# A two-layer decoder's attention phase: probabilities turned as half-height tiles ahead of the scores, and one score matmul for two key sets

## The reference

```python
q = (layernorm(x) @ wq + bq) / 8            # 16 heads x 64
k = concat(ctx @ wk + bk, mk)               # 128 token keys + 128 memory keys
v = concat(ctx @ wv + bv, mv)
x = x + softmax(q @ k.T) @ v @ wo + bo      # per sequence and head, fp32
```

## Time and profile before

| | us |
|---|---|
| median of 3 timed runs | 1543.92 |
| lowest and highest | 1542.75, 1546.67 |
| profiled execution, span | 1569.9 |
| TensorE busy in the span | 1397.6 (89%) |
| VectorE busy | 1162.8 (74%) |
| ScalarE busy | 1103.5 (70%) |
| GpSimd busy | 604.5 (39%) |

### The profile page before, as it was taken

How to read it: one execution, slowest core, us unless ns; L and a number is a source line. 1 busy time by engine, 2 the same in 40 slices (tenths; PEclk the granted TensorE clock), 3 DMA queues, 4 the chain that set the end, 5 groups by cost and what they waited for, 6 DMA issues and landing times.

```text
span 1569.9 us, 42930 instructions
## 1 busy us (share of the span) xinstructions
PE 1397.6 (89%) x15465; PEld 1050.6 (67%) x15465; DVE 1162.8 (74%) x2779; ACT 1103.5 (70%) x2899; POOL 604.5 (39%) x679
## 2 busy tenths in 40 slices
PE   2358999999999999999895899989989999999995
PEld 0124777777777777777674799856666667776663
DVE  3999879898888979776466344456688888887665
ACT  1126999889888988988794466647666776876652
POOL 0002423353443424210103535446655655544452
PEclk9999999999999999999998899989999999999996
DMA  6644141332214231011012332230101010000000
GB/s 173 157 101 95 42 102 49 77 73 76 57 52 99 52 96 47 15 46 45 14 35 61 94 91 79 62 123 16 29 12 35 12 38 9 23 22 3 22 9 14
DMA packets 82317, 88.63 MB, mean 56 GB/s; under 512 B 15296, under 2 KB 71488, under 8 KB 77504
## 3 DMA queue, kind: packets, MB, share of 16 engines
q1 hardware_dynamic: 74496, 73.65, 18.2%
q0 software_dynamic: 4096, 8.40, 1.8%
q10 hardware_dynamic: 3520, 3.84, 0.7%
HBM read 64.89 MB, written 17.83 MB: 53 GB/s over the span
## 4 chain that ended last, share of the span: by engine, by line
PE 71%; DVE 16%; issue 7%; ACT 3%; DMA 1%; ACTq 1%; SPq 0%; another core or an unknown queue 0%; DVEq 0%
PE P L1981 9%; PE P L898 7%; PE P L760 7%; PE P L744 5%; PE P L1514 4%; PE P L1481 4%; PE P L2045 3%; PE P L1999 3%; PE P L880 3%; PE P L746 3%; PE P L857 3%; PE P L868 3%; PE P L852 3%; PE P L1943 2%; PE P L2069 2%
## 5 line engine op out<-in xcount | busy, mean ns | idle before, releaser
L950 ACT ACTIVATE pr<-P,nm 128x256 f32<-128x256 f32 x512 | 237.7, 489 | 10.2 <-DVE nm L1122 10.2
L2193 ACT ACTIVATE et<-P 128x1024 f32<-128x1024 f32 x128 | 131.2, 1025 | 101.1 <-PE P L1988 100.9
L1122 DVE TENSOR_REDUCE nm<-P 128x4 f32<-128x1024 f32 x128 | 156.1, 1220 | 53.0 <-PE P L746 47.7
L352 POOL TENSOR_TENSOR rstd<-ve,mhalf 128x1 f32<-128x1 f32 (+2 forms) x81 | 75.9, 939 | 255.7 <-DVE ve L347 252.9
L934 ACT COPY ptS<-P 128x512 f32<-128x512 f32 x256 | 137.0, 586 | 40.3 <-PE P L760 33.7
L760 PE MATMUL P<-ident,pr 128*128 128x128 f32 x1024 | 141.4, 281 | 7.3 <-issue 3.3
L925 ACT ACTIVATE pr<-pr,ri 128x256 f32<-128x256 f32 x256 | 118.7, 522 | 26.4 <-DVE pr L1099 25.0
L744 PE MATMUL P<-kt_w,qt 64*128 64x128 f32 x1024 | 127.6, 311 | 4.5 <-ACT pr L950 4.3
L1573 ACT ACTIVATE hT<-P,mixing 128x128 f32<-128x128 f32 x284 | 81.4, 368 | 66.7 <-PE P L1481 59.6
L760 PEld LDWEIGHTS P<-ident,pr 128*128 128x128 f32 x1024 | 111.0, 142 | 24.2 <-issue 11.1
L664 POOL TENSOR_TENSOR kv_qk<-kv_qk,r_w 128x512 f32<-128x512 f32 x48 | 61.1, 1272 | 161.9 <-DVE pr L1099 115.7
(11 more groups left out here) (355 smaller groups left out, 4039.8 us busy)
## 6 DMA issues: line engine op xcount, KB each, us to landing
kv_qk<-scr_v SPq DMA_DIRECT2D x16, 1024.0 KB, 8.1
r_w<-scr_r SPq DMA_DIRECT2D x16, 1024.0 KB, 10.7
xt<-scr_xs SPq DMA_DIRECT2D x71, 64.0 KB, 1.8
scr_ys<-yt SPq DMA_DIRECT2D x71, 64.0 KB
x<-in_x SPq DMA_DIRECT2D x8, 256.0 KB, 9.7
scr_v<-mixing SPq DMA_DIRECT2D x8, 256.0 KB, 2.0
scr_r<-mixing SPq DMA_DIRECT2D x8, 256.0 KB, 2.0
xb<-in_x SPq DMA_DIRECT2D x8, 256.0 KB, 4.3
```

The costliest lines, as they stand in the source:

```text
L950: e = nc.scalar.activation(pr[:, s % 3, h * KEYS:(h + 1) * KEYS], scores(s)[:, h // 2, (h % 2) * KEYS:(h % 2 + 1) * KEYS], ACT.Exp, bias=n ...
L1122: nc.vector.tensor_reduce(nm[:, s % 3, 0:4].rearrange("p (a h) -> p a h", a=2), scores(s).rearrange("p a (h k) -> p a h k", k=KEYS), AX.X, ...
L2193: nc.scalar.activation(et[:, u % 4, :, :, :], scoresT, ACT.Exp).then_inc(S["h_exp"], 1)
```

## The change

1. On TensorE the transposes of unit s - 2 now come before the scores of unit s.
2. Each 128x128 transpose becomes two of 64x128 (queries 0 to 63, queries 64 to 127). The first half of all eight goes to bank 4, the second half to bank 5; the two semaphore steps come with the last pair.
3. ScalarE's two copies follow: each copies one half of the queries for all eight key blocks, from 8 x 64 columns in the bank to eight pieces of 64 in `ptS`.
4. `KT`'s chunks get 128 columns more, which hold the memory keys; `mkT` becomes a view of them. One matmul with a moving operand of two pieces (128 columns of tokens, 128 of memory) takes the place of two.
5. The experts' second weights use the first 4,096 words of the larger buffer.

```diff
-        r8_w1, kt_w2, qt = [sb_shared(n, E * F) for n in ("r8_w1", "kt_w2", "qt")]
+        r8_w1, qt = [sb_shared(n, E * F) for n in ("r8_w1", "qt")]
+        kt_w2 = sb_shared("kt_w2", 8 * (N + MEM))
...
-            KT = kt_w2.rearrange("p (c n) -> p c n", n=N)
+            KT = kt_w2.rearrange("p (c n) -> p c n", n=N + MEM)
+            mkT = KT[:, :, N:N + MEM]
...
-                    if 0 <= s < UNITS:
-                        g, hq, b = unit(s)
...
-                        for cc in range(2):
-                            for hh in range(2):
-                                bank = scores(s)[:, hh, :]
-                                part, c = slice(64 * hh, 64 * hh + 64), 2 * hq + cc
-                                q = QT[part, c, b * T:(b + 1) * T]
-                                nc.tensor.matmul(bank[:, cc * KEYS:cc * KEYS + T], q, KT[part, c, b * T:(b + 1) * T],
-                                                 start=True, stop=True)
-                                m = nc.tensor.matmul(bank[:, cc * KEYS + T:(cc + 1) * KEYS], q, mkT[part, c, :],
-                                                     start=True, stop=True)
-                        m.then_inc(S["b_s"], 1)
-
                     i = s - LAG_PT
...
                         for kb in range(2):
                             for h in range(4):
-                                m = nc.tensor.transpose(P[:, 4 + kb, h * T:(h + 1) * T],
-                                                        pr[:, i % 3, h * KEYS + kb * T:h * KEYS + (kb + 1) * T],
-                                                        ident[:, :])
-                            m.then_inc(S["b_pt"], 1)
+                                k = 4 * kb + h
+                                for half in range(2):
+                                    part = slice(64 * half, 64 * half + 64)
+                                    m = nc.tensor.transpose(P[:, 4 + half, 64 * k:64 * k + 64],
+                                                            pr[part, i % 3, h * KEYS + kb * T:h * KEYS + (kb + 1) * T],
+                                                            ident[part, part])
+                                    if k == 7:
+                                        m.then_inc(S["b_pt"], 1)
+
+                    if 0 <= s < UNITS:
+                        g, hq, b = unit(s)
...
+                        for cc in range(2):
+                            for hh in range(2):
+                                part, c = slice(64 * hh, 64 * hh + 64), 2 * hq + cc
+                                keys = KT[part, c, :].rearrange("p (m k) -> p m k", k=T)[:, b:GS + 1:GS - b, :]
+                                m = nc.tensor.matmul(scores(s)[:, hh, cc * KEYS:(cc + 1) * KEYS], QT[part, c, b * T:(b + 1) * T],
+                                                     keys, start=True, stop=True)
+                        m.then_inc(S["b_s"], 1)
...
-                        for kb in range(2):
-                            act.wait_ge(S["b_pt"], 2 * i + kb + 1)
-                            nc.scalar.copy(ptS[:, i % 2, kb * 512:(kb + 1) * 512], P[:, 4 + kb, :])\
-                              .then_inc(S["b_pts"], 1)
+                        for half in range(2):
+                            act.wait_ge(S["b_pt"], 2 * i + half + 1)
+                            nc.scalar.copy(ptS[:, i % 2, :].rearrange("p (k q) -> p k q", q=T)[:, :, 64 * half:64 * half + 64],
+                                           P[:, 4 + half, :].rearrange("p (k q) -> p k q", q=64)).then_inc(S["b_pts"], 1)
```

More of the change, by code:

```diff
@@ L447, in first_phase @@
             bv = sb1("bv", [128, H * DK])
-            mkT = sb1("mkT", [128, 8, MEM])
             mv = sb1("mv", [128, H * DK])
@@ L647, in sync_program @@
                             e0, e1 = half * E // 2, (half + 1) * E // 2
-                            sp.dma_start(units_of(kt_w2)[:, e0 * FC:e1 * FC, :],
+                            sp.dma_start(units_of(kt_w2[:, 0:E * F])[:, e0 * FC:e1 * FC, :],
                                          d["w2T"].rearrange("(u f) h -> f u h", f=128)[:, e0 * FC:e1 * FC, :])\
@@ L759, in tensor_program @@
                             for h in range(4):
-                                m = nc.tensor.transpose(P[:, 4 + kb, h * T:(h + 1) * T],
-                                                        pr[:, i % 3, h * KEYS + kb * T:h * KEYS + (kb + 1) * T],
-                                                        ident[:, :])
-                            m.then_inc(S["b_pt"], 1)
+                                k = 4 * kb + h
[8 more added lines that the diff above has]
+                        g, hq, b = unit(s)
+                        pe.wait_ge(S["b_q"], 8 * g + 2 * hq + 2)
+                        pe.wait_ge(S["b_k"], 8 * g + 2 * hq + 2)
+                        if s:
+                            pe.wait_ge(S["b_exp"], 2 * s - 1)
+                        for cc in range(2):
[5 more added lines that the diff above has]
+                        m.then_inc(S["b_s"], 1)
                     g = group_at(s, BANK7["norm"])
@@ L1016, in scalar_program @@
                             act.wait_ge(S["b_kp"], 8 * g + c + 1)
-                            nc.scalar.activation(KT[:, c, :], P[:, 3, :], ACT.Identity, bias=bqk[:, 1, c:c + 1])\
+                            nc.scalar.activation(KT[:, c, 0:N], P[:, 3, :], ACT.Identity, bias=bqk[:, 1, c:c + 1])\
                               .then_inc(S["b_k"], 1)
@@ L1349, in sb2 @@
                 return own.enter_context(nc.sbuf_tensor(name, shape, dt))
-            w1, w2, b1, b2 = r8_w1, kt_w2, mixing[:, 0:E * D], mixing[:, 8 * N:8 * N + E * D]
+            w1, w2, b1, b2 = r8_w1, kt_w2[:, 0:E * F], mixing[:, 0:E * D], mixing[:, 8 * N:8 * N + E * D]
             qS, kS, vD, xb, ya, yb, xnD, xTd, qkv, qkq, hn3 = homes
```

## The result

| | before | changed |
|---|---|---|
| median, us | 1544.24 | 1581.57 |
| lowest, highest | 1542.75, 1546.67 | 1580.05, 1582.76 |
| span of the profiled execution | 1569.9 | 1578.3 |

The ratio is 1.023, with a 95% interval of 1.022 to 1.025: 37 us slower. The forecast was 1615 us, slower by 71. The direction and the mechanism were right, and the size was twice too large.

The account below looks back on a forecast made before the run. TensorE bounds the kernel, with VectorE and ScalarE having little to spare. The new loop adds 60 us in groups 1 to 5, then +9, +4 and -2: 1543.9 + 71 = 1615 us, range 1572 to 1656.

Parts of the forecast that it names:

- the loop: First phase: VectorE's add holds up transposes, scores, reduction, then the next add; +71 us, chance 0.73.
- VectorE's legs of group 3 plus sixteen TensorE legs: Group 3's time: reduction start to next add's end (67.8 us), plus sixteen times add's end to reduction start (2.25): 103.8.
- Transposes, 0.89 us: TensorE, each unit: eight half-height loads in each half, side by side, at 0.111 us each.
- Half time: Rival: half-height transposes on TensorE take half the time because 64 rows load twice as quickly; 1577 us, chance 0.09.
- Taking turns: Rival: the array's two halves load in turn, so TensorE's transposes take 1.78 us; 1695 us, chance 0.06.
- Faster, TensorE stays the bound: Rival: VectorE's add is done before TensorE's slot begins, so only 0.12 us a slot is saved; 1529 us, chance 0.09.
- The signs: Expected first-phase trace: 6.3 to 6.7 us a slot, 50 us or more TensorE idle, busy share about 0.86.
- Scores, 0.12 us: TensorE's score matmuls per slot: 0.09 us saved on a restart, 0.03 from fewer, wider steps.
- TensorE's saving: TensorE's block of scores and transposes goes from 2.12 to 2.0 us, 0.12 us a slot saved.
- Copies: nothing: ScalarE's two copies per unit, now in pieces with gaps, were taken to cost nothing; upper bound 19 us a group.
- Groups 0, 6 and 7: First phase's first and last two groups of sixteen slots: +9, +4 and -2 us.

Follow-up runs that it names:

- e3: Changed kernel with VectorE's add from bank 4 moved from the head of its next slot into the same slot; ratio 1.000 to before.
- e9: Changed kernel with half tiles turned by an ordinary fp32 matmul with the identity instead of transpose mode; 1763.3 us where before takes 1546.4.
- e6: Kernel before with only the 256-column score matmuls and mkT inside KT; old order, transposes and copies; ratio 0.9925 to before.
- e2: Changed kernel with the scores first again, half-height transposes behind them; ratio 0.981 to before, 1541.1 against 1572.3 us.
- e8: The changed kernel itself, unaltered, run again in a later session; ratio 1.024 to before.
- e4: Changed kernel with the scores first again and VectorE's add from bank 4 made early; ratio 0.987 to before.
- e5: Changed kernel, scores first, transposes behind the query or key projection, probabilities times values ahead of bank 4's projection; ratio 1.038 to before.
- e10: Changed kernel with scores first again and the recurrent block's additions moved from VectorE to GpSimd from group 2 on; ratio 0.981 to before.
- e12: Changed kernel with scores first and transposes behind the bank 7 work, ahead of the query or key projection; ratio 0.989 to before.
- e7: Kernel before with only the half-height transposes and their copies; old order and scores; ratio 0.9875 to before.

## Why the prediction was right, and where its size was off

- *What bounds the kernel; the loop.* Right. e1, with nothing but the order changed, is 6.8% slower; e3, with nothing but the add moved, takes the change's 2.4% back.
- *The rule "VectorE's legs of group 3 plus sixteen TensorE legs".* Right within 1.5 us for legs of 1.92 to 3.22 us: 98.5 against 97.99 (leg 1.92), 108.6 against 107.27 (2.55), 119.3 against 120.74 (3.22). Two legs always make up a turn; what the rule claims, and the traces bear out, is that VectorE's part stays what it was: 67.0, 66.1 and 66.2 us for 67.8.
- *Transposes, 0.89 us.* The term that was mis-sized: 0.50. I took the pace of L825's ordinary loads, 0.111 us, for loads in transpose mode. The trace of before had the sign: a load of L760, in transpose mode, lasted 140 ns, although it has twice the rows of L744's, which lasted 187. In the 0.93 us of the eight transposes it was probably not the load that set the pace but their 128 moving columns, which the change halves. That is an estimate and not shown: in the changed kernel passes of 256 and 512 columns follow each other at 0.216 and 0.429 us, 0.84 ns a column, which would give 0.107 us for 128 columns and 0.054 for 64, where the transposes show 0.109 and 0.062. 0.39 us x 16 slots x 5 groups = 31 us, cut to 27 by what the leg really was (0.33 less): 60 - 27 = 33, which is what groups 1 to 5 show.
- *The rivals.* "Half time" gave 1577 us, close to the measured 1582, but its cause, loads of 64 rows twice as quick, is not what e9 shows. The Trainium skill, "TensorE: Matmul & The Clock Gate", section "LDWEIGHTS (loading the stationary operand)", says that a load's time goes with its columns and not its rows. By that rule, e9 agrees: 0.112 us for 64 rows against 0.111 for 128. The lower edge of the range was set by this rival, so that the result lies inside it is in part luck.
- *A rule read wrongly.* The prediction took the following rule for a promise that half-height loads are twice as quick. "TensorEngine Tiling (Array Packing)", section "Theoretical Speedup", in the Trainium skill, gives up to twice the speed for 64 rows. What doubles in e9 is not the pace of one half but the number of passes at work: its 32 half-height passes take 1.80 us, 0.056 us each, because two halves run side by side at 0.112. The change cuts each full-height tile in two, so it has twice as many tiles, and the doubling only makes up for that: sixteen full-height passes, two for each of the eight tiles, would take at L825's pace 16 x 0.111 = 1.78 us.
- *The other rivals.* "Taking turns" did not occur: in 0.60 us there were 16 loads. "Faster, TensorE stays the bound" holds for none of the groups 0 to 5; for groups 6 and 7 it stays open, since their +0.9 and -0.5 us are less than the "remote" waits in them.
- *The signs.* TensorE's busy share fell to about 0.86, as said. The waits put down to the two adds by name are 36.1 us, where 50 or more was said, and the rest of them stands under "issue". A slot takes 5.9 to 6.1 us, where 6.3 to 6.7 was said, and the maximum waits 0.8 us a slot for the scores, where it was 1.2: the same term again. The block of transposes and scores takes about 1.6 us (409.35 to 410.94), and the prediction had that down as the sign that the load goes with rows. By e9 the sign misleads: the mode and, probably, the columns give the same number. And the reading of the old waits was short: 2.9 + 0.6 us left out the 14.4 put to "issue".
- *Scores, 0.12 us.* Right: 1.18 forecast, 1.20 measured, and e6 gives 0.75%, 12 us for 128 slots of 0.09.
- *TensorE's saving.* Too small: 0.12 us for the block, where in e2 it goes from 2.12 us to 1.56 and the time falls by 1.9%. I kept the transposes' time in both places.
- *Copies: nothing.* Right for the changed order, 596 ns against 586.
- *Groups 0, 6 and 7.* +3.7, +0.9 and -0.5 us (e8 against the earlier trace rows) for +9, +4 and -2. A smaller leg works that way too; how much of it is that is not shown.
- *What sets the 5.38 us of e2* stays open. VectorE (80.6 of 86.1 us), ScalarE (79.2) and TensorE (83.2) are all near full, each of the moves tried (e4, e5, e10, e12) lost or did nothing, and none of them isolates one engine. No version is clearly faster than e2; e10 has the same ratio.

## What to carry to other kernels

When an instruction is moved ahead on an in-order engine, take all of its waits along: what stood in front of it was the cover of those waits, and what now stands behind it inherits them. If the awaited engine itself waits for one of those, the two legs of the loop add up, and the sum, not any engine's busy share, is the slot. Measure the pace of an operation on its own kind: take it from a row in the same mode, and look at whether the load or the moving columns set it.

## What the runs showed of the hardware

- An fp32 transpose of a 64x128 tile with 64 moving columns runs at 0.062 us in each half of the array's rows (8 in 0.50 us, both halves at once); the 128x128 one ran at 0.109. The load in this mode lasts 138 ns and keeps up with 0.062; an ordinary fp32 load of the same size lasts 188 ns and keeps a pace of 0.112. Whether the load or the 64 columns set the 0.062 was not tried apart.
- Some VectorE instructions are held up by a two-input addition on GpSimd (1.27 to 1.60 us). With two tensor inputs, 128x64 took 1.31 us in place of 0.25 and 128x256 1.49 in place of 0.42, ending 0.08 and 0.28 us after GpSimd's addition; with one tensor input, L1151 took 1.49 in place of 0.42. The Trainium skill, "VectorE: DVE Perf Modes", section "Two Vector instructions with no wait between them", says that VectorE's second SBUF read interface, which serves an instruction with two SBUF tensor inputs or in a two-port mode, is shared with GpSimd. The trace agrees in the two-input cases; in which mode L1151 ran, it does not show.
- The same program takes different times in different sessions (before: 1544 and 1546 us in some, 1572 and 1573 in others), and the number of the chip does not decide it: on chip 14 before took 1573 us in one session and 1546 in another. What the traces show is "remote" waits: 18 to 33 us of them, summed over the engines, in the profiled executions of before and e1 to e8, none in those of the changed kernel's first run and e9 to e12. The longest lasts 8.9 us (e7); what they wait for stays open, and so does how much of the 28 us they explain. Ratios within one session agree (1.023 and 1.024).
